# Fused attention, feed-forward and expert layers, 16 groups of 4 sequences: inputs laid out by the host, last two groups' banks and every engine's order rewritten

## The reference

```
x = x + attention(ctx, layernorm(x), mask, b)          # 8 heads of 16, keys = ctx[..., :128], values = ctx[..., 128:]
x = x + ffn(layernorm(x))                              # 256 -> 512 -> 512 -> 128, weights +-1, relu
x = x + hnet(layernorm(x), ctx, lens, W_in, g_res ...) # rmsnorm, 128x128 projection, picked context rows
x = x + moe(layernorm(x), W, b, Wg, bg)                # 8 experts of 128x128, softmax gate, top 2
```

## Time and profile before

| what | value |
|---|---|
| median of three runs | 539.25 us |
| the profiled execution's own time | 538.97 us |
| its span, first to last instruction | 537.2 us |
| PE busy | 497.7 us, 93% |
| DVE busy | 433.1 us, 81% |
| POOL busy | 364.5 us, 68% |
| ACT busy | 356.7 us, 66% |
| moved by DMA | 16.98 MB |

### The profile page before, as it was taken

The page is one execution under the profiler, slowest core; times in us unless marked ns, Lnnn a source line. Parts: engine busy times, 40 slices in busy tenths (PEclk is TensorE's granted clock), DMA queues, the critical chain, the costliest instruction groups (busy, mean ns, idle before and its releaser), DMA issues.

```text
span 537.2 us, 15110 instructions
## 1 busy us (share of the span) xinstructions
PE 497.7 (93%) x5549; PEld 324.0 (60%) x5549; DVE 433.1 (81%) x1404; ACT 356.7 (66%) x761; POOL 364.5 (68%) x633
## 2 busy tenths in 40 slices
PE   1756999999999999999999999999999999999893
PEld 1645565666656565766666566666666666655551
DVE  4735868899897979888897979799887785867897
ACT  3398698887967867677686866777566665655410
POOL 7644444588858869686868778686845857654865
PEclk9987899999999999999999999999999999999997
DMA  7402101010310101010110101000000000100010
GB/s 170 101 4 55 32 16 56 2 51 6 82 36 18 34 22 51 23 50 21 31 43 21 52 1 51 21 21 27 3 21 1 2 22 1 33 1 21 1 31 29
DMA packets 28503, 16.98 MB, mean 32 GB/s; under 512 B 3687, under 2 KB 28429, under 8 KB 28430
## 3 DMA queue, kind: packets, MB, share of 16 engines
q1 hardware_dynamic: 26670, 15.57, 10.5%
q10 hardware_dynamic: 1760, 0.46, 0.4%
HBM read 11.74 MB, written 4.24 MB: 30 GB/s over the span
## 4 chain that ended last, share of the span: by engine, by line
PE 64%; DVE 5%; issue 1%; ACT 0%; DVEq 0%
PE ps L2186 16%; PE ps L2134 16%; PE ps L2145 4%; PE ps L2079 4%; PE ps L2022 4%; PE ps L2096 4%; PE ps L2127 4%; PE ps L2164 2%; PE ps L2165 2%; PE ps L2104 2%; PE ps L2054 2%; PE ps L2177 2%; DVE weighed L1046 1%; PE ps L2083 1%; PE ps L2047 1%
## 5 line engine op out<-in xcount | busy, mean ns | idle before, releaser
L2186 PE MATMUL ps<-w_moeT,y4T 128*128 128x512 f32 x256 | 123.5, 607 | 1.2 <-DVE gd L1005 1.1
L613 POOL TENSOR_TENSOR sum<-weighed 128x512 f32<-128x512 f32 x60 | 76.1, 1269 | 71.2 <-DVE weighed L1046 71.2
L2134 PE MATMUL ps<-h,w 128*128 128x512 f16 x512 | 118.6, 379 | 0.0
L1638 ACT ACTIVATE h<-ps 128x512 f16<-128x512 f32 x128 | 74.1, 591 | 46.9 <-PE ps L2134 35.9
L1046 DVE TENSOR_TENSOR weighed<-ps,wgt 128x1024 f32<-128x1024 f32 x64 | 77.8, 1218 | 31.7 <-PE ps L2186 30.7
L969 DVE SCALAR_TENSOR_TENSOR h<-ps,h 128x512 f16<-128x512 f32 x128 | 85.6, 682 | 20.2 <-ACT h L1638 20.1
L2134 PEld LDWEIGHTS ps<-h,w 128*128 128x128 f16 x512 | 48.3, 98 | 56.2 <-issue 5.6
L1604 ACT ACTIVATE prT<-ps,maskT 77x1024 f32<-77x1024 f32 x64 | 67.3, 1101 | 14.8 <-PE ps L2083 14.5
L2186 PEld LDWEIGHTS ps<-w_moeT,y4T 128*128 128x128 f32 x256 | 45.1, 189 | 43.0 <-issue 35.0
L565 POOL TENSOR_TENSOR rs<-ve,neg_half 128x4 f32<-128x4 f32 x64 | 64.9, 1013 | 8.7
L560 POOL TENSOR_TENSOR ve<-mv,eps 128x4 f32<-128x4 f32 x64 | 14.2, 222 | 60.6 <-DVE mv L903 60.4
(11 more groups left out here) (171 smaller groups left out, 986.1 us busy)
## 6 DMA issues: line engine op xcount, KB each, us to landing
cx<-in_ctx SPq DMA_DIRECT2D x16, 308.0 KB
xa<-in_x SPq DMA_DIRECT2D x16, 256.0 KB, 3.0
out_x<-xo SPq DMA_DIRECT2D x16, 256.0 KB, 2.3
plugs<-plug_d SPq DMA_DIRECT2D x16, 77.0 KB
nat<-in_L_ffn_W SPq DMA_DIRECT2D x1, 512.0 KB
k_u<-in_L_ffn_k ACTq DMA_DIRECT2D x1, 256.0 KB, 3.9
k_u<-in_L_ffn_k ACTq DMA_DIRECT2D x1, 128.0 KB, 3.4
k_u<-in_L_ffn_k ACTq DMA_DIRECT2D x1, 64.0 KB, 4.6
```

Of the source, the lines that this page charges most:

```text
L613: nc.gpsimd.tensor_tensor(sum4[:], both[:, 0:4 * D], both[:, 4 * D:8 * D], ALU.add).then_inc(c_sum4.sem, 1)
L1638: last = nc.scalar.activation(h[:, 0, (k - 1) % FC, :], src, ACT.Relu)
L2134: last = pe.matmul(pb(g, k), w2[:, i, c * 128:(c + 1) * 128], h1[:, g.p, part, i, :], start=(i == 0 and part == 0), stop=(i == FC - 1 and ...
L2186: last = pe.matmul(pm(g, j)[:, half, :], y4T[:, g.p, j * S:(j + 1) * S], w_moeT[:, half * 512:(half + 1) * 512], start=True, stop=True)
```

## The change

The function `kernel()` now rearranges the inputs in numpy ahead of the launch (`laid_out`) and the result behind it. Rows, context and output are grouped so that each partition's part is one run of memory (2048 bytes for rows and output, 4096 for the context). New inputs are `keys` (turned, each head's other half zeroed, as `kT` holds them), `values` (as `vx` holds them, ones included), `mask_turned`, and `weights` (all ten blocks turned, side by side) with one row `biases`. So `a_turn_keys`, `a_keys`, `a_values_in`, `make_values`, `turn_mask`, `take_mask`, `turn_weights` and `take_weights` are gone, and SyncE has three loads a group for the context where it had one. The query copy takes the factor that the key copies had. POOL now subtracts the weights' last row in place (`make_sums_zero`).

```diff
             def load_keys(g):
+                if g.has(2):
+                    sp.wait_ge(a_less[1].sem, a_less[1].of(g, back=2))
+                sp.dma_start(kT[:, g.p], keys[g.n]).then_inc(keys_in[g.p].sem, 16)
+            def load_values(g):
+                if g.has(2):
+                    sp.wait_ge(a_pv.sem, a_pv.of(g, back=2))
+                sp.dma_start(vx[:, g.p], values[g.n]).then_inc(values_in[g.p].sem, 16)
+            def load_context(g):
                 if g.has(4):
-                    sp.wait_ge(a_cT.sem, a_cT.of(g, back=4))
-                    sp.wait_ge(a_vx.sem, a_vx.of(g, back=4))
                     sp.wait_ge(a_hp0.sem, a_hp0.of(g, back=4))
                     sp.wait_ge(a_ss.sem, a_ss.of(g, back=4))
...
             load_rows(g[0])
             load_masks()
+            load_context(g[0])
             load_rows(g[1])
             load_keys(g[0])
             mask_rows()
+            load_context(g[1])
+            load_values(g[0])
             load_keys(g[1])
+            load_context(g[2])
             load_weights()
-            load_keys(g[2])
+            order_counts()
             load_rows(g[2])
             load_rows(g[3])
+            load_keys(g[2])
+            load_rows(g[4])
```

```diff
-            a_turn_keys(g[0])
             turn_ends()
             a_turn_rows(g[0])
             a_scores(g[0], 0)
+            a_turn_rows(g[1])
+            a_scores(g[0], 1, (a_max[0], g[0]))
             count_ends((s_ends, g[0]))
...
+            a_weights(g[0], 1, (a_prT[0], g[0]))
             a_scores(g[1], 1, (a_max[0], g[1]))
-            a_weights(g[0], 1, (a_prT[0], g[0]))
-            turn_weights((a_max[1], g[1]))
             a_values(g[0])
-            a_turn_maxima(g[1], (s_weights, g[0]))
-            a_turn_keys(g[2], (a_prT[1], g[0]))
-            a_weights(g[1], 0)
+            a_turn_rows(g[2], (a_prT[1], g[0]))
+            a_turn_maxima(g[1], (a_max[1], g[1]))
             a_turn_out(g[0])
```

```diff
+            return {NG - 2: ("gpsimd", "vector", "gpsimd", "vector"), NG - 1: ("gpsimd", "scalar", "vector", "vector")}.get(g.n, ("gpsimd",) * G)
...
+            def e_accumulate(g, j, half):
+                for e in range(4 * half, 4 * half + 4):
+                    so_far = xo if e else xd
+                    if e:
+                        dve.wait_ge(v_step.sem, v_steps(g, j) + e)
+                    last = nc.vector.scalar_tensor_tensor(xo[:, g.p, cols], pm(g, j)[:, e // 4, (e % 4) * D:(e % 4 + 1) * D],
+                                                          wgt[:, g.p, j, e:e + 1], so_far[:, g.p, cols], ALU.mult, ALU.add)
...
             b_layer(g[15], 8)
-            e_experts(g[13], 2, (c_weighed, g[13], 1))
+            e_experts(g[13], 1, (a_prT[1], g[15]))
             b_last(g[15])
+            e_experts(g[13], 2, (c_weighed, g[13], 1))
             d_turns(g[14], (c_yT, g[14]))
             e_experts(g[13], 3, (c_weighed, g[13], 2))
             d_gate_scores(g[14], (c_x3, g[14]))
             e_experts(g[14], 0, (c_weighed, g[13], 3))
-            keep_busy(3, 1, (b_x2, g[15]))
             c_turns(g[15], (b_lo, g[15], 9))
-            keep_busy(3, 1)
             c_project(g[15], (b_x2, g[15]))
             e_experts(g[14], 1, (c_weighed, g[13], 4))
...
+            e_sum(g[15], 1, (s_weighed, g[15], 2))
```

More of the change, by code:

```diff
@@ new lines, in count, with place, place_free @@
+        def count(kind, g, j):
+            return sum(1 for i, k in sums_of if how(i)[k] in kind and (i.n, k) <= (g.n, j))
+        def place(g, j):
+            return buffered.index((g.n, j)) % 2
+        def place_free(g, j):
+            n, k = buffered[buffered.index((g.n, j)) - 2]
+            if how(Group(n))[k] == "scalar":
+                return s_sum.sem, s_sum.of(Group(n), k + 1)
+            return c_sum4.sem, added(Group(n), k)
+        def added(g, j):
+            return count(("gpsimd",), g, j)
@@ L457, in _ @@
             plug(g[4])
[L458 to L471 removed]
+            store(g[0])
+            load_values(g[6])
+            plug(g[5])
@@ new lines, in _ @@
+            load_rows(g[8])
+            load_context(g[7])
+            store(g[1])
+            load_keys(g[7])
+            load_context(g[8])
+            plug(g[6])
+            load_values(g[7])
+            load_rows(g[9])
+            load_context(g[9])
+            plug(g[7])
+            load_keys(g[8])
+            load_context(g[10])
+            load_rows(g[10])
+            load_keys(g[9])
+            store(g[2])
+            load_values(g[8])
+            store(g[3])
+            load_values(g[9])
@@ new lines, in _ @@
+            plug(g[8])
+            load_rows(g[11])
+            load_context(g[11])
+            load_keys(g[10])
+            load_context(g[12])
+            load_values(g[10])
+            store(g[4])
+            load_rows(g[12])
+            load_keys(g[11])
+            plug(g[9])
+            load_rows(g[13])
+            plug(g[10])
+            store(g[5])
+            load_keys(g[12])
+            plug(g[11])
+            load_values(g[11])
+            store(g[6])
+            load_context(g[13])
@@ new lines, in normalise_rest @@
+            def normalise_rest(ln, g, src):
+                n, p = ln.n, g.p
+                dve.wait_ge(ln.rs.sem, ln.rs.of(g))
+                dve.wait_ge(ln.turned.sem, ln.turned_at(g, back=2))
+                for j in range(2, G):
+                    last = nc.vector.tensor_scalar(xn[n][:, p, j * D:(j + 1) * D], src[:, j * D:(j + 1) * D],
+                                                   mv[n][:, p, j, 0:1], rs[n][:, p, j:j + 1], ALU.subtract, ALU.mult)
+                last.then_inc(ln_rest[n].sem, 1)
```

1393 lines of the change are left out of this document (741 added, 652 removed).

## The result

The changed kernel takes 552.3 us (median of 4 runs, 551.07 to 553.35), the kernel before 539.27 beside it: 1.0236 times the time, 95% interval 1.0205 to 1.0266. It is 2.4% slower, where 525.5 with 515 to 534 was forecast and "slower" had a chance of 0.04. The profiled execution took 553.35 us for a span of 550.6.

A forecast was written before the change was run, and what follows sets the result against it. PE was taken to bound the middle, the first group's chain the start, DVE's list the end. Gains of 4.0 (start), 4.6 (middle) and 5.0 (end) summed to 13.6, giving 525.5 us, range 515 to 534.

The forecast's parts named there:

- (b): Start: rows of groups 2 and 3 issued behind the counts' trip, landed near 30, first division at 38 instead of 43.3.
- a loss of 2 if the counts' trip through a queue full of 4 MB takes 6 us more: Start: lower bound of its effect, where a gain of 4 us was taken and 9 was the upper bound.
- (a): Start: mark_ends and four normalising instructions stand ahead of the first maxima on DVE, 16.6 instead of 15.2; price 1.4 us.
- (c): Start: ACT normalises group 0 ahead of group 1's second exponential, and PE waits for both; cost 2.1 us.
- 0.5 to 1 us of the earlier scores: Start: first scores begin that much earlier than now, added to 3.2 to give a gain of 4 us.
- 0.35 a group: Middle: PE time saved by not turning keys, for 13 groups 4.6 us (3.5 to 6.0).
- The new orders of all lists I cost at zero: Middle: PE's cover of 3.7 us idle should be kept; if kept less well, 0 to 6 us more.
- rival 1: Start and middle: orders cost more than they save, start gives 0, PE idles 3 us more; 532.4 us, chance 0.22.
- Rival 4: Middle: keys land late and stop PE once in each of some 12 groups; slower, 545.6 us, chance 0.04.
- 3.7 less 1: End, behind the last projection: DVE's net gain of 3.7 us, with 1 left for its wait at the last gate.
- 0.02 to start the dependent next: End: added to 0.29 us for each dependent summing step on DVE, giving 0.31.
- rival 3: End: the clock falls and the last four expert steps take 13.8 instead of 6.9 us; 533.5 us, chance 0.07.

The follow-up runs named there:

- both: Changed kernel with the 127-row load split into 112 and 15 rows and the counts' store moved behind the loads of rows: 534.2 us, ratio 0.9909.
- fixed_dve_order: both, with VectorE's order altered in two middle periods (maxima split ahead of the first layer's step, pick behind the third expert's weighing): 529.81 us, ratio 0.9824.
- split_weights: Changed kernel with only the 127-row load of turned weights split into 112 and 15 rows: 534.92 us, ratio 0.9932.
- fixed_key_turns: both, with four unused transposes a group put back on TensorE for groups 4 to 15: 536.84 us, ratio 0.9944.
- counts_later: Changed kernel with the counts written and read back behind the loads of rows 2 and 3, the 127-row load kept: 549.82 us, ratio 1.0203.
- before_127: Kernel before, with its 128-row load of expert weights made in 127 rows and one: 550.11 us, ratio 1.0201.
- fixed_both_orders: both, with the altered orders of fixed_dve_order and of fixed_start_order together: 529.31 us, ratio 0.9812.
- fixed_start_order: both, with the start's order altered on TensorE, VectorE and ScalarE, group 0's out-turn ahead of group 2's rows: 534.91 us, ratio 0.9899.
- no_chain: fixed_dve_order, with VectorE's summing steps for four experts made independent, leaving out the sum: 529.24 us, ratio 0.9818.

## Why the prediction was wrong, step by step

Times at five landmarks in us: first layer, last layer of groups 0 and 12, end of the last projection, end of VectorE's last instruction. The fourth is the start of the experts behind it.

| kernel | layer | g0 | g12 | projection | end |
|---|---|---|---|---|---|
| before | 52.32 | 72.49 | 426.76 | 512.09 | 534.33 |
| changed | 66.74 | 86.94 | 443.83 | 525.60 | 548.01 |
| mended (`both`) | 49.42 | 69.62 | 424.89 | 508.26 | 529.35 |
| `fixed_dve_order` | 48.98 | 68.62 | 420.92 | 502.69 | 525.09 |

**The step that failed.** It is (b) of the start, "I place the issue near 23 and the rows' at 27, landed near 30", with "a loss of 2 if the counts' trip through a queue full of 4 MB takes 6 us more" as the lower bound. The rows went out at 42.21. The trip had been taken as a matter of bytes and order; how many engines a load is spread over was not asked, though the diff has `w_T[0:D - 1, :]`. The start lost 14.4 us instead of gaining 4.0, and `split_weights` gives 17.4 back. No rival had this mechanism. The rule of the Trainium skill cited above speaks straight against the edit, and it was not weighed.

**The start without it** gains 52.32 - 49.42 = 2.9 where 4.0 was forecast; the first layer at 49.4 misses "46 to 49" by little. (a) was about right: from the first scores to the first maxima it took 1.1 us longer (12.08 to 14.73 against 13.65 to 15.20), where 1.4 was priced. The division came at 38.60, gaining 4.7 of the 5.3, and from there to the first layer 1.8 were lost (10.82 us against 9.02), where (c) put 2.1. What was wrong in the sum is the "0.5 to 1 us of the earlier scores": it was added to a division that had been placed at an absolute time, and so couldn't come on top.

**The middle.** 0.35 a group, forecast as 4.6 in sum, was 0.24 on the mean by `fixed_key_turns`, under its lower bound of 0.27; that the slow changeover stays is the likely reason, not shown. From group 0's to group 12's last layer `before` takes 354.27, and the new order has one expert step of 1.72 more in that stretch, so 355.99 is the like for like. The changed kernel takes 356.89, the mended one 355.27, `fixed_dve_order` 352.30. "The new orders of all lists I cost at zero" failed: two places of VectorE's list make PE wait 2.51 and 1.19 us and cost 3.0 (355.27 - 352.30), inside the 0 to 6 that were set aside but not in the sum. With these two mended the gain is 3.7. So rival 1, whose price held 3 us of idle PE in the middle, came true there. In the changed kernel PE also ran at 0.94 of the clock from 135 to 165 us, behind the longer wait. The doubled traffic was hidden, as forecast: behind the first scores no wait of PE ends with a DMA, and keys land in 3.4 us. Rival 4 didn't occur.

**The end.** Up to the last projection the changed kernel gains (512.09 - 426.76) - (525.60 - 443.83) = 3.6 from group 12's last layer on. Less the 1.7 of the expert step that moved ahead of it, 1.9 are left, where 2.3 were forecast: a little over-sized (all key turns lie ahead of group 12's last layer). Behind the projection 3.7 less 1 was forecast, and it took 22.41 us instead of 22.24. Two terms failed. The summing step was mis-sized: 0.31 taken, 0.38 measured, 4 x 8 x 0.07 = 2.2 us; the text's own "with 0.40 2.9 less" covers it. The "0.02 to start the dependent next" was wrong by kind: the wait costs 0.12 over the unchained 0.26, and a size between two rows can't show it. And rival 3 came true in small: the last experts ran partly at the low clock in this profile, and VectorE waited 1.19 us for them. The changed kernel's end:

```profile
534.53 8.81 PE L2359 MATMUL ps<-w_T,y4T 128*128 128x512 f32 x16
...
541.72 0.35 DVE L1200 SCALAR_TENSOR_TENSOR xo<-ps,wgt,xd 128x128 f32<-128x128 f32 x1 [1.19 <-PE ps L2359]
542.10 2.67 DVE L1200 SCALAR_TENSOR_TENSOR xo<-ps,wgt,xo 128x128 f32<-128x128 f32 x7
```

In `both` the same 16 matmuls take 7.11 us and this part 21.09; there the clock fell a period earlier instead (group 14's to 15's last layer 22.6 us against 21.0). What makes it fall in one place and not the other isn't settled. The missing fillers may well have a part in it: of the 13 profiles of kernels without the 17 matmuls at the end 8 have a low clock between 470 us and the last expert matmul, of the 5 with them none. The sum had put that at nothing, and rival 3 had 0.07. But no experiment shows it: with them back the median is no lower, and they cost 0.3 us themselves where the clock holds.

Sum for the mended kernel: 2.9 + 0.7 + 0.2 + 1.2 = 5.0 of 13.6, with the expert step counted in the stretch where it now stands.

Two sums of the prediction are off by themselves, and neither changed the forecast: with a step of 0.19 the gain would be 3.8 more (4 x 8 x 0.12), not 6.8, and rival 4's total is 545.4, not 545.6.

## What to carry to other kernels

Read each new load's slowest dimension: 127 rows made one engine of sixteen carry half a megabyte, and every issue behind it on the queue waited, small ones too. Cut such a load at a multiple of 16 rows, as 112 and 15 here. A new order of a list is no free edit where another engine's cover is thin: look for short steps that an edit puts beside GpSimd's long ones, ahead of a step that TensorE waits for. Chained small steps, each waiting for the one before, started 0.38 us apart instead of 0.26; alternate two chains where the sum allows.

## What the runs showed of the hardware that was not expected

- A load over one DMA engine holds the queue that issued it: the next issue took 12.63 us (changed), 14.22 (`counts_later`), and two took 26.97 (`before_127`), against 0.3 to 0.4 for an ordinary one. Rows of 4.5 KB moved at 25 GB/s, pieces of 512 bytes at 20.
- The landing of one small store moves from profile to profile with the same code ahead of it: PE waited 2.0 to 6.9 us for the mask's row in ten profiles. Issued behind fewer loads it was 0.8 to 1.8 in six.
- The granted clock differs between profiles of the same start. In 30 to 60 us it was 0.58 in `fixed_both_orders` and 0.94 in `fixed_start_order`, 0.83 in `fixed_dve_order` and 0.60 in `no_chain`, each pair with the same lists there. What decides isn't shown, so one profile of a start says little about its clock.
